# Attention on the first core of a pair: transposing the divided exponentials by DMA instead of on TensorE

## The reference, cut to what matters

```python
xn = _layernorm(x)                                # x: 4 x 2048 x 2048
q, k, v = jnp.split(xn @ w_atten.T, 3, axis=2)    # 16 heads of 128
q = apply_rope(q, rope); k = apply_rope(k, rope)
att = jnp.einsum('bhqd,bhkd->bhqk', q, k) / sqrt(128)
att = jax.nn.softmax(jnp.where(causal, att, -inf), axis=-1)
y = jnp.einsum('bhqk,bhkd->bhqd', att, v)
s = y @ w_proj.T
h = silu(xn @ w_gate) * (xn @ w_up)               # 8192 wide
g = silu(sparsify_2to4(h) @ w_down)               # keep the 2 largest of each 4
out = x + s * g
```

## Time and profile before

| | us |
|---|---|
| three runs: lowest, median, highest | 2223.14, 2280.35, 2400.09 |
| the profiled execution's own time | 2221.76 |
| its span (core 0, the slowest) | 2220.2 |
| spans of the other first cores | 2218.5 to 2219.4 |
| spans of the second cores | 2147.8 to 2149.1 |
| TensorE busy on core 0 | 2153.6 (97%) |
| VectorE busy, ScalarE busy | 854.8 (39%), 658.2 (30%) |

### The profile page before, as it was taken

One profiled execution on the slowest core, in us unless ns is written; L12 is line 12 of the kernel. 1 busy time (PEld: TensorE's weight loads), 2 busy tenths in 40 slices (PEclk: granted clock), 3 DMA queues, 4 the chain that ended last, 5 costly groups with the idle time before them and its releaser, 6 DMA issues.

```text
span 2220.2 us, 41255 instructions; the slowest of 8 cores (2147.8 to 2220.2 us)
## 1 busy us (share of the span) xinstructions
PE 2153.6 (97%) x14592; PEld 1357.3 (61%) x14640; DVE 854.8 (39%) x1543; ACT 658.2 (30%) x1442; POOL 136.7 (6%) x260
## 2 busy tenths in 40 slices
PE   4899999999999999999999999999999999999998
PEld 3566666776666666666666666666665666666665
DVE  5567776667610133444443333444443111110111
ACT  4455555555531222222222222222222000000000
POOL 0000000000000000000000000000000000000000
PEclk9999999999999999999999999999999999999999
DMA  9333443322356534343433445354544876655661
GB/s 251 72 61 58 78 75 60 74 57 52 71 128 145 103 62 76 58 77 59 75 67 68 70 86 97 79 98 81 96 80 90 273 155 131 132 120 114 134 131 44
DMA packets 95201, 213.13 MB, mean 96 GB/s; under 512 B 11154, under 2 KB 60306, under 8 KB 93330
## 3 DMA queue, kind: packets, MB, share of 16 engines
q0 software_dynamic: 36864, 134.23, 36.2%
q1 hardware_dynamic: 57170, 75.59, 10.6%
q10 hardware_dynamic: 960, 0.59, 0.1%
HBM read 306.84 MB, written 28.31 MB: 151 GB/s over the span
## 4 chain that ended last, share of the span: by engine, by line
PE 93%; DVE 3%; issue 2%; DMA 1%; ACT 0%; DVEq 0%; SPq 0%; ACTq 0%
PE ps L646 43%; PE ps L664 23%; PE ps L515 9%; PE ps L616 6%; PE ps L503 5%; PE ps L572 2%; PE ps L560 2%; PE ps L491 1%; PE ps L546 1%; DMA arena<-xN 1%; DVE arena L892 1%; DVE arena L861 0%; PE ps L548 0%; DVE arena L837 0%; DMA arena<-arena 0%
## 5 line engine op out<-in xcount | busy, mean ns | idle before, releaser
L646 PE MATMUL ps<-arena 128*128 128x384 bf16 x5952 | 967.4, 326 | 0.0
L646 PEld LDWEIGHTS ps<-arena 128*128 128x128 bf16 x5952 | 582.4, 98 | 384.8
L664 PE MATMUL ps<-arena 128*128 128x384 bf16 x3072 | 500.8, 327 | 2.5 <-DVE arena L970 2.5
L664 PEld LDWEIGHTS ps<-arena 128*128 128x128 bf16 x3072 | 300.9, 98 | 202.4 <-issue 4.5
L970 DVE TENSOR_TENSOR arena<-arena,ps 128x384 f32<-128x384 f32 x186 | 102.8, 553 | 659.8 <-PE ps L646 633.3
L515 PE MATMUL ps<-arena 128*128 128x384 bf16 x1536 | 281.4, 329 | 0.4 <-issue 0.3
L805 ACT ACTIVATE arena<-arena 128x384 f32<-128x384 f32 x192 | 100.5, 523 | 607.4 <-DVE arena L970 607.4
L515 PEld LDWEIGHTS ps<-arena 128*128 128x128 bf16 x1536 | 143.7, 99 | 79.1 <-issue 4.0
L977 DVE TENSOR_TENSOR arena<-arena 128x384 f32<-128x384 f32 x48 | 26.8, 559 | 426.5 <-ACT arena L820 416.0
L820 ACT ACTIVATE arena<-ps 128x384 f32<-128x384 f32 x48 | 23.6, 491 | 476.9 <-PE ps L664 471.2
L892 DVE TENSOR_REDUCE arena<-ps 128x1 f32<-128x128 f32 (+2 forms) x144 | 118.2, 821 | 94.0 <-PE ps L548 94.0
(11 more groups left out here) (51 smaller groups left out, 1168.8 us busy)
## 6 DMA issues: line engine op xcount, KB each, us to landing
arena<-wgu POOLq DMA_DIRECT2D x128, 512.0 KB, 6.2
arena<-wd POOLq DMA_DIRECT2D x64, 512.0 KB, 6.1
arena<-wqkv POOLq DMA_DIRECT2D x48, 512.0 KB, 6.4
arena<-xN SPq DMA_DIRECT2D x9, 1024.0 KB, 12.0
d_s<-arena SPq DMA_DIRECT2D x48, 192.0 KB, 2.8
d_hT<-arena SPq DMA_DIRECT2D x24, 384.0 KB, 5.9
arena<-d_hT SPq DMA_DIRECT2D x4, 2304.0 KB, 18.0
arena<-d_s SPq DMA_DIRECT2D x48, 192.0 KB, 4.9
```

What stands on the lines that cost most here:

```text
L646: mm = e.matmul(ps[2 * b + up][:, 0:P.tw], w[:, f, :], M.xn_own[:, f, t * P.tw:(t + 1) * P.tw], start=(f == 0), stop=(f == NF - 1))
L664: mm = e.matmul(ps[P.nt * (fc % P.fcs) + t][:, 0:P.tw], w[:, j, :], M.hT[16 * q + j][:, t * P.tw:(t + 1) * P.tw], start=(q == 0 and j == 0 ...
```

## The change

All of it is in the first core's program, except that `k2` and `q2` change their list in the plan of the first core:

- `turn_p` and `leave_p` are gone on the first core. SP issues for every window one DMA transpose from `pbf` to `pT` (`turn` in `prog_sync`), after `divide(w)` (`v_nr`).
- `pbf` has three buffers, `pT` five; `divide(w)` waits for the transpose of w-3, the transpose of w for `values(w-5)`.
- `values` follows its window by four instead of two (`pvlag`), and `leave_y` too. It waits for the transpose (`dT0` to `dT2`) instead of `a_te`.
- The rope's halves are swapped by two ScalarE copies of 64 partitions behind each k or q eviction, in place of the two DMAs.
- The blocks of a head come in the order 0, 1, 2, 4, 5, 6, 7, 3, 8 instead of 0, 1, 4, 5, 6, 7, 2, 3, 8; `banks` follows.
- The units `k2` and `q2` of head 0 move from the end of stage 1 into the filler.
- At the tail `values(140)` and `values(141)` come ahead of the first projections, and `values(143)` behind the third.

```diff
+        self.npb = 3 if self.ahead else 1
+        self.npt = 5 if self.ahead else 2
+        self.pvlag = 4 if self.ahead else 2
-        self.order = [0, 1, 4, 5, 6, 7, 2, 3, 8] if self.ahead else list(range(self.nb))
+        self.order = [0, 1, 2, 4, 5, 6, 7, 3, 8] if self.ahead else list(range(self.nb))
@@ plan of the first core
-            late = ["v3", "v4"]
+            late = ["k2", "q2", "v3", "v4"]
-        if not p:
-            self.start += ["k2", "q2"]
@@ prog_sync
+        def turn(w):
+            n = P.blocks(w)
+            e.wait_ge(S["v_nr"], w + 1)
+            if w >= P.npt:
+                e.wait_ge(S["p_pv"], w - P.npt + 1)
+            e.dma_start_transpose(out=M.pT[w % P.npt][:, 0:n, :],
+                                  in_=M.pbf[w % 3][:, 0:128 * n]).then_inc(S[f"dT{w % 3}"], 16)
         for w in range(P.nw + 1):
-            for u in P.early[w] + P.late[w]:
-                if u in P.rope_no:
-                    swap(P.rope_no[u])
+            if P.ahead and w < P.nw:
+                turn(w)
@@ prog_tensor
             if P.ahead:
-                if w >= 2:
-                    turn_p(w - 2)
                 steps(P.parts[w][0])
-                if w >= 2:
-                    values(w - 2)
+                if w >= P.pvlag:
+                    values(w - P.pvlag)
@@ prog_tensor, values
-            e.wait_ge(S["a_te"], w + 1)
+            if P.ahead:
+                e.wait_ge(S[f"dT{w % 3}"], 16 * (w // 3 + 1))
@@ prog_scalar, leave
                 e.copy(M.raw[b][:, 0:cols], bank[:, 0:cols]).then_inc(S["a_u"])
+                if P.ahead:
+                    e.wait_ge(S["a_u"], u + 1)
+                    if r >= P.nraw:
+                        e.wait_ge(S["v_t2"], r - P.nraw + 1)
+                    e.copy(M.xsw[b][0:64, 0:cols], M.raw[b][64:128, 0:cols]).then_inc(S["a_sw"])
+                    e.copy(M.xsw[b][64:128, 0:cols], M.raw[b][0:64, 0:cols]).then_inc(S["a_sw"])
@@ prog_vector, divide
-            if w >= P.npe:
-                e.wait_ge(S["p_t"], w + 1 - P.npe)
+            if P.ahead and w >= 3:
+                e.wait_ge(S[f"dT{w % 3}"], 16 * (w // 3))
```

More of the change, by code:

```diff
@@ L90, in __init__ @@
         self.npe = 2 if self.ahead else 1
-        self.order = [0, 1, 4, 5, 6, 7, 2, 3, 8] if self.ahead else list(range(self.nb))
-        self.banks = [[0, 2, 0, 3, 0, 2, 0, 2, 0], [3, 0, 2, 0, 2, 0, 2, 0, 1]] if self.ahead else [[0] * self.nb] * 2
+        self.npb = 3 if self.ahead else 1
+        self.npt = 5 if self.ahead else 2
+        self.pvlag = 4 if self.ahead else 2
+        self.order = [0, 1, 2, 4, 5, 6, 7, 3, 8] if self.ahead else list(range(self.nb))
+        self.banks = [[0, 2, 0, 3, 2, 0, 2, 0, 0], [3, 0, 2, 0, 0, 2, 0, 2, 1]] if self.ahead else [[0] * self.nb] * 2
         self.lag = 2 if self.ahead else 1
@@ L256, in __init__ @@
         self.pexp = [A.alloc(P.keys) for _ in range(P.npe)]
-        self.pbf = [A.alloc(P.keys // 2, BF16) for _ in range(P.npe)]
+        self.pbf = [A.alloc(P.keys // 2, BF16) for _ in range(min(P.npb, 2))]
         if P.p:
@@ L267, in __init__ @@
             self.pT = [A.alloc(P.keys // 2, BF16).rearrange("p (k x) -> p k x", x=128) for _ in range(2)]
+            self.pbf.append(A.alloc(P.keys // 2, BF16))
         kw = max(w for _, w in P.kt)
@@ L272, in __init__ @@
         self.t2 = A.alloc(kw)
+        if P.p == 0:
+            assert A.ptr <= RING
+            for i in range(3):
+                A.ptr = WORK + 4 * tw * i
+                self.pT.append(A.alloc(P.keys // 2, BF16).rearrange("p (k x) -> p k x", x=128))
         A.ptr = PEXP if P.p else WORK
@@ L425, in prog_sync @@
                 e.dma_start(out=M.rsin[:], in_=ropeS[:, 0:P.keys]).then_inc(S["dRS"], 16)
-        for w in range(P.nw + 1):
-            for u in P.early[w] + P.late[w]:
-                if u in P.rope_no:
-                    swap(P.rope_no[u])
+        def turn(w):
[5 more added lines that the diff above has]
+                                  in_=M.pbf[w % 3][:, 0:128 * n]).then_inc(S[f"dT{w % 3}"], 16)
+        for w in range(P.nw + 1):
+            if P.ahead and w < P.nw:
+                turn(w)
+            elif not P.ahead:
+                for u in P.early[w] + P.late[w]:
+                    if u in P.rope_no:
+                        swap(P.rope_no[u])
         for k in range(16 * P.nt):
@@ L559, in turn_p @@
                     e.wait_ge(S["a_y"], w)
-                mm = e.transpose(psT[:, k, :], M.pbf[w % P.npe][:, k * 128:(k + 1) * 128], M.id[:])
+                mm = e.transpose(psT[:, k, :], M.pbf[w % P.npb][:, k * 128:(k + 1) * 128], M.id[:])
             mm.then_inc(S["p_t"])
@@ L565, in values @@
             h, n = w // P.nb, P.blocks(w)
-            e.wait_ge(S["a_te"], w + 1)
+            if P.ahead:
+                e.wait_ge(S[f"dT{w % 3}"], 16 * (w // 3 + 1))
+            else:
+                e.wait_ge(S["a_te"], w + 1)
             if w:
@@ L620, in prog_tensor @@
         if P.ahead:
-            turn_p(P.nw - 2)
+            values(P.nw - 4)
+            values(P.nw - 3)
             project(0)
@@ L624, in prog_tensor @@
             project(1)
-            turn_p(P.nw - 1)
             project(2)
+            values(P.nw - 1)
         else:
@@ L630, in prog_tensor @@
             turn_p(P.nw - 1)
-        values(P.nw - 1)
+            values(P.nw - 1)
         for k in range(3 if P.ahead else 1, 16 * P.nt):
@@ L691, in leave @@
                     e.wait_ge(S["v_t1"], r - P.nraw + 1)
-                    e.wait_ge(S[f"dSW{b}"], 32 * (r // P.nraw))
+                    if P.ahead:
+                        e.wait_ge(S["a_sw"], 2 * (r - P.nraw + 1))
+                    else:
+                        e.wait_ge(S[f"dSW{b}"], 32 * (r // P.nraw))
                 e.copy(M.raw[b][:, 0:cols], bank[:, 0:cols]).then_inc(S["a_u"])
-                if u < P.nstart:
+                if P.ahead:
+                    e.wait_ge(S["a_u"], u + 1)
[3 more added lines that the diff above has]
+                    e.copy(M.xsw[b][64:128, 0:cols], M.raw[b][0:64, 0:cols]).then_inc(S["a_sw"])
+                elif u < P.nstart:
                     e.wait_ge(S["a_u"], u + 1)
@@ L756, in prog_scalar @@
         for w in range(P.nw):
-            if w >= 2 and P.ahead:
-                leave_p(w - 2)
-            elif w >= 2:
+            if w >= 2 and not P.ahead:
                 leave_y(w - 2)
@@ L770, in prog_scalar @@
                          bias=nm[w % 2][:], scale=SCALE, accum_out=den[w % 2][:]).then_inc(S["a_ex"])
-            if P.ahead and w >= 2:
-                leave_y(w - 2)
+            if P.ahead and w >= P.pvlag:
+                leave_y(w - P.pvlag)
             elif w and not P.ahead:
@@ L784, in prog_scalar @@
         if P.ahead:
-            leave_p(P.nw - 2)
+            leave_y(P.nw - 4)
+            leave_y(P.nw - 3)
         leave_y(P.nw - 2)
-        leave_p(P.nw - 1)
+        if not P.ahead:
+            leave_p(P.nw - 1)
         leave_y(P.nw - 1)
@@ L835, in rope @@
             e.tensor_tensor(M.t1[:, 0:n], M.raw[b][:, 0:n], M.rcos[:, tok:tok + n], ALU.mult).then_inc(S["v_t1"])
-            e.wait_ge(S[f"dSW{b}"], 32 * (r // P.nraw + 1))
+            if P.ahead:
+                e.wait_ge(S["a_sw"], 2 * (r + 1))
+            else:
+                e.wait_ge(S[f"dSW{b}"], 32 * (r // P.nraw + 1))
             e.tensor_tensor(M.t2[:, 0:n], M.xsw[b][:, 0:n], M.rsin[:, tok:tok + n], ALU.mult).then_inc(S["v_t2"])
@@ L906, in divide @@
             e.wait_ge(S["v_rc"], w + 1)
-            if w >= P.npe:
-                e.wait_ge(S["p_t"], w + 1 - P.npe)
-            e.tensor_scalar_mul(M.pbf[w % P.npe][:, 0:n], M.pexp[w % P.npe][:, 0:n],
+            if P.ahead and w >= 3:
+                e.wait_ge(S[f"dT{w % 3}"], 16 * (w // 3))
+            elif w and not P.ahead:
+                e.wait_ge(S["p_t"], w)
+            e.tensor_scalar_mul(M.pbf[w % P.npb][:, 0:n], M.pexp[w % P.npe][:, 0:n],
                                 rc[b][:, 0:1]).then_inc(S["v_nr"])
```

6 lines of the change are left out of this document (3 added, 3 removed).

## The result

The change makes the kernel faster by 1.5%: the ratio of the times is 0.9846, with a 95% interval of 0.9809 to 0.9883. The profiled execution took 2186.9 us, where 2159 was forecast and 2221.76 stood before; its span is 2185.3. So 35 us came of the 63 that were forecast. The runs of the changed kernel have a median of 2192.05 and go up to 2255.11; a run near the top is one in which a die ran slower, and these are left out of the ratio.

A forecast was written before the change was run, and what follows sets the result against it. The first core bounds the kernel, in its windows TensorE with its work and waits. 2221.8 - 40.0 - 29 - 6.4 + 14 = 2160 us, 2159 with the tail's waits gone; range 2148 to 2207.

The forecast's parts named there:

- Transposes off TensorE, -40.0: In the windows, 720 transposes of 0.0555 us leave TensorE: -40.0 us, sure as long as the chain follows TensorE.
- The spread waits, -29: TensorE's waits before turn_p and values, 30 us spread over the windows, go: -29 us, bounds 0 to -30.
- rival B: TensorE's spread 30 us of waits stay, before scores or values: 2175 to 2206 us; chance 0.21 together with a no-change case.
- The sign by which B was to be known: In the trace, TensorE's waits before scores over 30 us would show that waits had only changed hands.
- What hid the transposes: In the windows, values follows four windows later, giving each DMA transpose some 7 us to land; landing expected under 5 us.
- The rule for the path: For DMA transposes in the windows, the nearest row was a 48 KB copy within SBUF, landing in 2.3 us.
- VectorE, +14: In seven k and q stretches VectorE falls 4.4 us behind, about 2 us lost in each: +14 us, bounds 0 to +31.
- The seam, -6.4: Before window 2, TensorE's 6.37 us wait for window 0's exponential goes, by ScalarE swaps and units made filler: -6.4 us.
- Swaps on ScalarE at no cost: In the windows, two copies for each of 96 units add 95 us to ScalarE, leave_p removes 99.9: cost nothing.
- The sum: For the profiled execution, 2221.8 us with all terms and the tail's waits of 0.3 and 0.5 us gives 2159 us.
- The floor, rival A: VectorE's lag is absorbed, core 0 comes to 2145 us and the second core sets the time, 2150; chance 0.15.

The follow-up runs named there:

- 3: The changed kernel with DMA transposes of one block only from window 45 on, the rest left out: ratio 0.9840 to the kernel before, mean span 2182.2 us.
- 10: The changed kernel with bf16 rope products and, from window 45 on, one-block transposes, the rest left out: ratio 0.9702 to the kernel before, windows 479.6 us.
- 11: The changed kernel with bf16 rope products and projection weight pieces from the eighth on cut to 256 of 2048 columns: ratio 0.9705 to the kernel before.
- 7: The changed kernel with the rope's two products in bf16 on the first core, nothing left out: ratio 0.9737 to the kernel before, windows 488.1 us.
- 5: The kernel before with 510 of 720 TensorE transposes left out and no DMA transposes: ratio 0.9929 to the kernel before, mean span 2208.2 us.
- Experiment 1: The changed kernel with the result of values alternating between two PSUM banks on the first core: 2180.0 and 2184.5 us, no interval.
- 4: The changed kernel with k2 and q2 of head 0 back at the end of stage 1: ratio 0.9861 to the kernel before, mean span 2185.8 us.
- 9: The changed kernel with the rope's halves swapped by DMA, in the windows behind the transposes in SP's queue: ratio 0.9956 to the kernel before.
- 12: The changed kernel with k2 and q2 back at the end of stage 1 and the old block order: ratio 0.9873 to the kernel before.

## Why the prediction was right and wrong, step by step

- **Transposes off TensorE, -40.0.** Right as a count: no such matmuls are left. The span fell by 34.9 us, less than this term alone, so all that the other terms gave was taken back elsewhere.
- **The spread waits, -29: wrong, and this is the step that failed.** They left `turn_p` and the copy, but waits of `values` for its PSUM bank and for late transposes took their place, 26 us on core 0 and 29 on core 4 in the rows. By the count of the windows, 40.1 us of waits and slow matmuls stand on core 4, where 36.5 stood before and 36.5 - 29 - 6.4 + 14 = 15 were forecast. This is rival B (waits change hands, 2175 to 2206), which the result falls into. It had named waits "before scores" or "before `values`"; they came before `values`, and before scores there is one of 2.2 us. The sign by which B was to be known, over 30 us before scores, would have missed it.
- **What hid the transposes: wrong.** "All of these times fit the 7 us" went by the landing of single copies and pieces. Beside a weight piece a landing takes up to 10.3 us, and the cover does not always have 7: on core 4 the division ends 7.0 us behind the mask of its window in the mean and 10.5 at most. Price: 0 while VectorE is late (3), some 8.5 us once it is not (10 and 11). The rule for the path, the copy within SBUF, was near for the median: 3.7 us against 2.3. The page that gives 1309 ns a block (the Trainium skill, VectorE: DVE Perf Modes, The three transpose paths) would, read as throughput, have made the windows DMA-bound. 144 transposes went through windows of 3.6 us, so as a throughput it is not borne out.
- **VectorE, +14:** the mechanism was right, the size too small: taking most of it away is worth 22 us of the windows (7). The loss does not need the DMA: a kernel without DMA transposes gives back 12 to 14 of 28 us as well (5). The path was wrong. The prediction asked when `scores(w+2)` needs the exponential, 3.8 us of slack; but on ScalarE the eviction of y stands behind the exponential, and the next `values` needs it half a window earlier, 1.7 us less. Experiment 1 shows that this was not the whole either: a late division issues a late transpose.
- **The seam, -6.4.** The old wait went, by ScalarE's copies and not by moving the units (4, 9, 12). It was 5.4 to 6.4 us by core; core 0 had the longest. A new one of 2.2 us came with the two moved units. The slow matmuls behind it, some 1.7 us lost, are no new loss, since some 1.3 us were lost behind the old wait too. So -3 to -4 came of the -6.4.
- **Swaps on ScalarE at no cost: right,** and undervalued. The prediction had no term for what they save in the windows. With DMA swaps behind the transposes, the rest of the change gains 10 us by the ratio, instead of 34 (9).
- **The sum.** 2159 was forecast for the profiled execution and 2186.9 came. The windows say where the difference lies. Forecast were 472.7 us of work and 15.1 of waits, 487.8; the mean of the first cores is 510.5, so 22.7 us too much. Of these 8.4 are the VectorE term (22.4 for 14), 8.5 the late transposes (for 0), and the other 6 are waits that stay with both out of the way: 479.6 us (10) against the 472.7 of work, where 1 us was forecast. Part of these 6 has not been traced. The floor, rival A, was reached only there.

What stays open: a remedy for the late transposes that leaves nothing out was not tried, nor were the two buffers more that a longer lag of `values` would need.

## What to carry to other kernels

When work leaves the bounding engine, compare the shortened period with the busiest passes of the next engine, stretch by stretch, and test it cheaply: cut the same work out of the old kernel and see how much of it is gained (here 15 of 28 us). A cover of n periods for a DMA is measured from the late end of its producer and must hold for the slowest landing beside the largest transfer, not for the median. In an in-order queue, price a delay by everything behind it (here an eviction behind an exponential), not only by the consumer you have in mind.

## What the runs showed of the hardware that was not expected

- A DMA transpose of 1 to 9 blocks of 128x128 bf16 holds SP's queue for 1.12 to 3.11 us (median 1.21), where the plain 48 KB copies of the kernel before held it for 0.46 and 0.60 (medians of L414 and L415). With one block it is still 1.10 us:

```profile
L440 SPq DMA_TRANSPOSE arena<-arena x96: 1093/1096/1902, 252.3 to 583.2; - x96
DMA to landing us min/median/max: 2.2/2.5/8.2
```

- It costs the DMA engines more than its bytes. In the change the hardware queue moves 90.34 MB for 16.1% of the span of 16 engines, before 75.59 MB for 10.6%: 14.8 MB net for 117 us of all engines, 126 GB/s, where the 75.59 MB before went at 321.

```profile
q1 hardware_dynamic: 57170, 75.59, 10.6%
q1 hardware_dynamic: 139538, 90.34, 16.1%
```

- A ScalarE copy of 64 partitions and 384 columns (0.51 us) takes as long as the cast of 128 partitions and 384 columns in the earlier trace rows (0.495). Two halves cost double.
- A wait of 2.2 us was already followed by slow matmuls (the seam, granted clock 0.61), and one of 7.6 us by some 6 us at 1.2 GHz (0.64 over 8 us), so TensorE's waits cost more than their rows show.
